# Second feed-forward layer as three rounded products, with its input split on GpSimd, in a four-phase layer

## The chip, the cores and the metric

One Trainium2 chip, one of its cores. The metric is the device time of one execution in microseconds, the median of several runs. A profiled execution gives a trace: each instruction's start and length on TensorE (PE), VectorE (DVE), ScalarE (ACT), GpSimd (POOL) and the DMA queue of SyncE (SP).

## The reference

The input is 16 batches of 1024 tokens of 256 numbers. Four residual blocks follow one another, each behind a layer norm: a state-space layer, the feed-forward block, an attention layer, the feed-forward block again. The change is in the feed-forward block only:

```python
    gf = _global_net(x.mean(axis=1, keepdims=True), ...)   # one number per batch
    out = x
    for _ in range(3):
        h = _gelu(out @ w1 + b1)      # 256 -> 256
        h = _gelu(h @ w2 + b2)        # 256 -> 128, the layer that is changed
        h = _gelu(h @ w3 + b3)        # 128 -> 64
        tf = sigmoid(h @ w4 + b4)     # 64 -> 1
        coupling = 0.1 + adaptive_range * (0.7 * gf + 0.3 * tf - 0.5) * 2.0
        out = out + coupling * _twist(out)
```

`_twist` permutes the four quarters of a token's vector and changes two signs, so the kernel keeps `out @ w1` (u) and `twist(out) @ w1` (v) beside one another and rotates those two from cycle to cycle instead of multiplying by `w1` again.

## The kernel before

Each feed-forward phase runs 8 steps; a step takes two batches, cut into four chunks of 512 tokens (`CHAINS` = 4, the `c` of the code). Three cycles of four chunks make 12 slots a step (`SLOTS`, the `m` of the code); slot m is chunk m % 4 in cycle m // 4. Two slots make a pair. All engines run instruction streams that are written out in the order of `step`, and meet at counting semaphores. Each engine takes its instructions strictly in order.

A slot goes as follows. TensorE turns u with eight transposes into `turned_ps` (`turn`, L1088). ScalarE applies Gelu to its two halves (`gelu1`, L976) into `h1[k]`, one of two buffers. TensorE multiplies by w2 in full float32 (`layer2`, L1097; a float32 product is issued as two instructions, so there are four a slot), and ScalarE applies the second Gelu (`gelu2`, L968). For each pair of slots there follow `layer3` (L1106), `gelu3` (L953), `layer4` (L1115), `tanh` (L960) and, on VectorE, `couple` (L804 to L814). Behind it VectorE rotates u and v of the two chunks with `rotate` (L823) and in the first cycle `rotate_other` (L832), eight instructions each a pair; the next cycle's `turn` of those chunks waits for it. After `turn` of slot m TensorE can run at most one second layer behind.

In slots 2 to 9 the step also prepares the next step's four chunks, one in two slots: `turn_z` (L1057), `high` on ScalarE and `low` on VectorE (L791), which split the normalised input into a rounded part and a rest, then `both_products` (L1072): 24 products of rounded (fp32r) operands, three terms for each half of the 256 inputs and each of four tiles. The products stand at the end of slots 3, 5, 7 and 9.

GpSimd computes scale factors (`rstds`, L691 to L695) from VectorE's `measure`, products of the couplings (`after_two`, L702 to L705), and, when the third coupling of a pair of chunks is known, the combined factors (L713 to L721) and the part of the output that the input itself gives (`base`, L727 and four tensor_scalars of 128x256 at L729 for each chunk). VectorE's `finish` (L844, L846) adds the rest, and SP stores. `base` of chunks 2 and 3, and `finish` of all four, stand in the next step. Before the change `base(it, s, j)` did the combination and both chunks of pair j in one go. SP's queue holds stores and loads in a written order, two chunks at a time.

`moments` and `std` have three sets of buffers for chunk 0 and two for the others; VectorE waits for `base` of the step that used the set before (L771).

Of the kernel before, what the change touches and what calls it, by code (L numbers as in the profile page):

```python
# [10 lines left out]
F32 = mybir.dt.float32  # L11
# [495 lines left out]
def ffn_semaphores(sem):  # L507
# [3 lines left out]
             "turned h1_ready h2_done h2_ready h3_done h3_ready token_done token_ready "  # L511
# [6 lines left out]
def ffn_phase(nc, sem, shared, start, name, identf, x1, x2, cn, gc, adaptive_range, early=None):  # L518
# [10 lines left out]
    with ExitStack() as ctx:  # L529
# [6 lines left out]
        def sems(names):  # L536
# [24 lines left out]
        zT_hi_other, zT_lo_other = sb("zT_hi_other", [P, KT, CH], F32R), sb("zT_lo_other", [P, KT, CH], F32R)  # L561
        h1 = [sb(f"h1_{k}", [P, KT, CH]) for k in range(2)]
        h2 = [sb(f"h2_{k}", [P, CH]) for k in range(2)]
        h3 = sb("h3", [P, CH])
        stats = [sb(f"stats{k}", [P, TT, 6]) for k in range(2)]
        moments = [[sb(f"moments{s}_{c}", [P, TT, 2]) for s in range(3 if c == 0 else 2)] for c in range(CHAINS)]
        std = [[sb(f"std{s}_{c}", [P, TT]) for s in range(3 if c == 0 else 2)] for c in range(CHAINS)]
# [24 lines left out]
         turned, h1_ready, h2_done, h2_ready, h3_done, h3_ready, token_done, token_ready,  # L592
         global_done, global_ready, kappa_pos, kappa_ready, coupling_ready, rotated,
         prod_ready, a_two_ready, prods_ready, b_pos_ready, a_std_ready, base_ready, y_ready) = counted
        w1_loaded, loaded, const_ready, weights_rounded, weights_ready, columns_ready = sems(
            "w1_loaded loaded const_ready weights_rounded weights_ready columns_ready")
# [35 lines left out]
        with nc.Block() as block:  # L632
# [45 lines left out]
            def _(pool):  # L678
# [29 lines left out]
                def base(it, s, j):  # L708
# [14 lines left out]
                    for k in range(2):  # L723
                        c = 2 * j + k
                        if not isinstance(it, int) or it > start:
                            pool.wait_ge(y_stored[c], 16 * it)
                        g.tensor_tensor(base_carrier[:, c:c + 1], base_ones[:, :], base_ones[:, :], ALU.mult)  # L727
                        for t in range(TT):
                            last = g.tensor_scalar(y[c][:, t, :], of_batch(z0, it, c)[:, t, :], a_std[j][:, t, k:k + 1],  # L729
                                                   of_batch(moments, it, c)[:, t, 0:1], ALU.mult, ALU.add)  # L730
                        last.then_inc(base_ready, 1)

                def step(it, s, first, second_last, last):
                    if first:
                        rstds(it + 1, 1 - s, 0)
                    if not last:
                        rstds(it + 1, 1 - s, 1)
                    if not first:
                        base(it - 1, 1 - s, 1)
                    if not last:  # L740
                        rstds(it + 1, 1 - s, 2)
                        rstds(it + 1, 1 - s, 3)
# [1477 lines left out]
```

## Time and profile before

| | |
|---|---|
| median of 3 runs | 3763.09 us (3757.67 to 3768.05) |
| profiled execution | 3763.16 us; span of its instructions 3761.3 us |
| mean granted TensorE clock, whole span | 0.978 |
| busy, share of the span | TensorE 95%, VectorE 79%, ScalarE 58%, GpSimd 44% |
| feed-forward phases | about 390 to 990 us and 3175 to 3758 us of the span |

"Busy" is the union of an engine's instructions in a stretch; the profile's length of a matmul overlaps that of the next one, so the price of a block of matmuls is read from the starts of two blocks. A granted clock of 1.00 is the full 2.4 GHz.

### The profile page before, as it was taken

To read this page: it belongs to the slowest core of one execution; us is meant where nothing else is said; L and a number is where in the kernel's file an instruction comes from. 1 tells how busy PE (TensorE), PEld (TensorE's weight loads), DVE (VectorE), ACT (ScalarE), POOL (GpSimd) and SP (SyncE) were. 2 spreads that over 40 slices of the span, in tenths; PEclk is the share of its full clock that TensorE was granted. 3 is DMA by queue.
4 is the path that set the end of the run, shared out by engine and by line. 5 is a ranking of instruction groups with operands and counts; after the bars stand their busy time and mean duration, and the time that the engine had idled before them with its cause. 6 is when DMAs were issued, how large, how long until landed. Compare 5 with 4: busy or idle time off the path is not lost. (4 is left out here: it accounts for less than half of the span.)

```text
span 3761.3 us, 76026 instructions
## 1 busy us (share of the span) xinstructions
PE 3560.0 (95%) x25550; PEld 2347.9 (62%) x25550; DVE 2952.9 (79%) x9275; ACT 2183.7 (58%) x4151; POOL 1666.4 (44%) x2027
## 2 busy tenths in 40 slices
PE   6999899999689999999999999999999998999997
PEld 5888666666455665566656656655666555666664
DVE  8998666766688888888888888888888893676775
ACT  1110456655337766766676667667667665656654
POOL 2332123223345556656555565565565511223323
PEclk9999899999879999999999999999999999999999
DMA  2333112111497978787887879788887832121211
GB/s 74 100 98 109 57 46 68 54 59 35 116 140 111 126 115 129 120 127 123 122 127 119 132 116 126 116 119 123 124 134 121 120 41 80 40 68 46 68 46 45
DMA packets 694291, 361.16 MB, mean 96 GB/s; under 512 B 297905, under 2 KB 660913, under 8 KB 693937
## 3 DMA queue, kind: packets, MB, share of 16 engines
q1 hardware_dynamic: 693936, 356.62, 53.5%
q8 instruction: 200, 3.28, 0.4%
q14 instruction: 155, 1.26, 0.2%
HBM read 204.49 MB, written 150.99 MB: 95 GB/s over the span
## 5 line engine op out<-in xcount | busy, mean ns | idle before, releaser
L1862 ACT ACTIVATE att_probs<-att_s 128x512 f32<-128x512 f32 x2304 | 1212.5, 601 | 461.2 <-PE att_s L2001 234.4
L1737 DVE CUSTOM_DVE_ANT_0 att_s<-att_s,att_above 128x384 f32<-128x384 f32 (+3 forms) x2048 | 950.2, 519 | 132.8 <-PE att_s L1981 127.1
L1981 PE MATMUL att_s<-att_ks,att_qs 48*128 48x512 f32 (+3 forms) x3072 | 896.0, 401 | 5.7 <-DVE att_maxima L1740 3.6
L2001 PE MATMUL att_s<-att_qs,att_ks 49*128 49x512 f32 (+3 forms) x3072 | 852.4, 373 | 20.5 <-DVE att_maxima L1737 5.2
L2001 PEld LDWEIGHTS att_s<-att_qs,att_ks 49*128 49x128 f32 x3072 | 487.6, 186 | 464.0 <-ACT att_probs L1862 271.6
L1740 DVE TENSOR_REDUCE att_maxima<-att_s 128x1 f32<-128x512 f32 x1024 | 661.9, 684 | 98.3 <-PE att_s L1981 93.2
L2029 PE MATMUL att_o_ps<-att_probs,att_vs 128*32 128x512 f32 (+3 forms) x6144 | 620.5, 497 | 25.1 <-ACT att_probs L1862 22.1
L1981 PEld LDWEIGHTS att_s<-att_ks,att_qs 48*128 48x128 f32 x3072 | 485.9, 189 | 26.4 <-DVE att_maxima L1737 8.9
L1097 PE MATMUL ffn_h2p<-ffn_h,ffn_w 128*128 128x512 f32 x768 | 365.0, 598 | 3.0 <-ACT ffn_h L968 0.9
L1951 PE MATMUL att_s<-att_mask,att_places 64*128 64x128 bf16 (+1 forms) x2560 | 327.7, 212 | 0.0
L1737 DVE DVE_READ_ACCUMULATOR2_ANT att_maxima<- 128x1 f32 x2048 | 293.0, 143 | 0.0
L946 ACT ACTIVATE ffn_uv<-ffn_uvp 128x512 f32<-128x512 f32 x256 | 153.1, 598 | 237.5 <-PE ffn_uvp L1072 237.5
L2029 PEld LDWEIGHTS att_o_ps<-att_probs,att_vs 128*32 128x32 f32 x6144 | 145.9, 108 | 222.9 <-issue 159.6
L1564 POOL CAST att_qs<-att_staged 113x1024 fp32r<-113x1024 f32 x128 | 253.7, 2005 | 0.0
L976 ACT ACTIVATE ffn_h<-ffn_turned,ffn_b 128x512 f32<-128x512 f32 x384 | 241.9, 684 | 13.5 <-PE ffn_turned L1088 11.6
L1564 POOL CAST att_ks<-att_staged 113x1024 fp32r<-113x1024 f32 x126 | 249.7, 2000 | 0.0
L968 ACT ACTIVATE ffn_h<-ffn_h2p,ffn_b 128x512 f32<-128x512 f32 x192 | 132.0, 687 | 197.8 <-PE ffn_h2p L1097 197.8
L1088 PEld LDWEIGHTS ffn_turned<-identf,ffn_uv 128*128 128x128 f32 x1536 | 174.8, 142 | 75.5 <-issue 53.9
L158 ACT ACTIVATE ssm_xnT<-ssm_turned 128x512 fp32r<-128x512 f32 x64 | 34.9, 595 | 313.7 <-PE ssm_turned L166 313.7
L1088 PE MATMUL ffn_turned<-identf,ffn_uv 128*128 128x128 f32 x1536 | 201.8, 274 | 10.2 <-DVE ffn_uv L823 8.0
L823 DVE SCALAR_TENSOR_TENSOR ffn_uv<-ffn_uv,ffn_c_pos 128x256 f32<-128x256 f32 x512 | 209.3, 483 | 2.3
L691 POOL TENSOR_TENSOR ffn_var_eps<-ffn_moments,ffn_eps 128x4 f32<-128x4 f32 x64 | 13.3, 208 | 433.4 <-DVE ffn_moments L776 433.4
(292 smaller groups left out, 6384.8 us busy)
## 6 DMA issues: line engine op xcount, KB each, us to landing
att_staged<-qk_scratch SPq DMA_DIRECT2D x768, 128.0 KB, 7.6
qk_scratch<-att_parts SPq DMA_DIRECT2D x128, 512.0 KB, 3.4
ffn_x<-x SPq DMA_DIRECT2D x64, 512.0 KB, 5.2
ssm_x<-in_L_attn_a_x_dram SPq DMA_DIRECT2D x32, 512.0 KB, 3.7
x<-ssm_y SPq DMA_DIRECT2D x32, 512.0 KB, 3.0
x<-ffn_y SPq DMA_DIRECT2D x32, 512.0 KB, 2.9
att_x<-x SPq DMA_DIRECT2D x32, 512.0 KB, 7.4
v_scratch<-att_v_tok SPq DMA_DIRECT2D x32, 512.0 KB, 5.3
```

The costliest lines, as they stand in the source:

```text
L823: last = v.scalar_tensor_tensor(out=new[:, t, 0:D], in0=old[:, t, D:2 * D], scalar=c_pos[i][j][:, t, k:k + 1], in1=old[:, t, 0:D], op0=ALU ...
L976: last = a(h1[k][:, f, :], turned_ps[:, f, :], ACT.Gelu, bias=b1[:, f:f + 1])
L1088: last = pe.transpose(turned_ps[:, f, t * P:(t + 1) * P], of[:, t, f * P:(f + 1) * P], identf[:, :])
L1097: last = mm(h2_ps[:, :], w2[:, f, :], h1[k][:, f, :], start=(f == 0), stop=(f == KT - 1))
L1564: last = g.tensor_copy(stack[0:ROWS, :].rearrange("p (t c) -> p t c", c=HD)[:, e * n:(e + 1) * n, :], staged[side][0:ROWS, :, e * n:(e + 1 ...
L1737: last = v.tensor_tensor_reduce(scores, scores, above[:, CH - w:CH], 1.0, -3.0e38, ALU.add, ALU.max, to)
L1740: last = v.tensor_reduce(to, scores, AX.X, ALU.max)
L1862: a(probs[u % PROBS][2 * g + p][:, 0:n], bank[:, 0:n], ACT.Exp).then_inc(exp_done, 1)
L1951: last = mm(blocks[:, at, GROUP * half:GROUP * (half + 1)], places[rows, 2 * (1 - k) + half, :], mask[rows, 1 - k, 0:len(cols), :], start= ...
L1981: last = mm(bank[:, col:col + w], rows_of(qs[buf], g, KROWS, p, BT * blk, BT * (blk + 1)), rows_of(ks[buf], g, KROWS, p, t0, t1), start=k ...
L2001: last = mm(bank[:, col:col + w], rows_of(ks[buf], g, SHIFT + 1, p, BT * j, BT * (j + 1)), rows_of(qs[buf], g, SHIFT + 1, p, t0, t1), star ...
L2029: last = mm(o_ps[32 * i:32 * i + 32, HD * (t0 - first_t):HD * (t1 - first_t)], vs[s][:, NBLK * head + j, :], probs[of % PROBS][i][:, col:c ...
```

## The change

The second layer becomes three rounded products, as the first already is: w2 is split once into `w2_hi` and `w2_lo` (two VectorE instructions before the first step), and h1 into `h1_hi` and `h1_lo` in every slot. For the first half of h1, ScalarE writes Gelu twice, once in float32 and once rounded. For the second half, GpSimd copies the float32 values into the rounded tile. GpSimd subtracts to give both low parts. A second layer is then six products instead of four instructions. GpSimd's order is written anew, with a split in every slot and the former `base` cut into `combine` and one `base` for each chunk. On TensorE `turn` comes ahead of `layer3` and `layer2`; ScalarE follows. On VectorE `finish` of chunk 1 and `normalise` of chunk 1 come two slots later, and `moments` and `std` get a third set for chunk 1.

```diff
@@ GpSimd @@
-                def base(it, s, j):
+                def combine(it, j):
...
                     pool.wait_ge(a_std_ready, n + 1)
-                    for k in range(2):
-                        c = 2 * j + k
...
+                def base(it, c):
+                    j, k = c // 2, c % 2
+                    if not isinstance(it, int) or it > start:
+                        pool.wait_ge(y_stored[c], 16 * it)
+                    g.tensor_tensor(base_carrier[:, c:c + 1], base_ones[:, :], base_ones[:, :], ALU.mult)
+                    for t in range(TT):
+                        last = g.tensor_scalar(y[c][:, t, :], of_batch(z0, it, c)[:, t, :], a_std[j][:, t, k:k + 1],
+                                               of_batch(moments, it, c)[:, t, 0:1], ALU.mult, ALU.add)
+                    last.then_inc(base_ready, 1)
+                def split(it, m):
+                    g1, k = SLOTS * it + m, m % 2
+                    for f in range(KT):
+                        if f == 0:
+                            pool.wait_ge(h1_high_ready, g1 + 1)
+                            if g1 >= 2:
+                                pool.wait_ge(h2_done, g1 - 1)
+                        else:
+                            pool.wait_ge(h1_ready, g1 + 1)
+                            g.tensor_copy(h1_hi[k][:, f, :], h1[k][:, f, :]).then_inc(h1_split, 1)
+                            pool.wait_ge(h1_split, 3 * g1 + 2)
+                        g.tensor_tensor(h1_lo[k][:, f, :], h1[k][:, f, :], h1_hi[k][:, f, :].bitcast(F32),
+                                        ALU.subtract).then_inc(h1_split, 1)
                 def step(it, s, first, second_last, last):
...
+                    for m in range(SLOTS):
+                        split(it, m)
+                        if m == 0 and not last:
+                            rstds(it + 1, 1 - s, 1)
+                        if m == 0 and not first:
+                            base(it - 1, 1)
+                        if m == 1 and not first:
+                            combine(it - 1, 1)
+                            base(it - 1, 2)
+                        if m == 2 and not first:
+                            base(it - 1, 3)
+                        if m in (4, 6) and not last:
+                            rstds(it + 1, 1 - s, m // 2)
+                        if m in (7, 9):
+                            after_two(it, (m - 7) // 2)
+                        if m == 10 and not second_last:
+                            rstds(it + 2, s, 0)
+                    combine(it, 0)
+                    base(it, 0)
@@ VectorE @@
-                        if m == 0 and not first:
+                        if m == 2 and not first:
                             finish(it - 1, 1 - s, 1)
...
-                        if m == 1 and not last:
+                        if m == 3 and not last:
                             normalise(it + 1, 1 - s, 1)
...
+                v.tensor_copy(w2_hi[:, :, :], w2[:, :, :]).then_inc(w2_rounded, 1)
...
+                v.tensor_tensor(w2_lo[:, :, :], w2[:, :, :], w2_hi[:, :, :].bitcast(F32), ALU.subtract).then_inc(columns_ready, 1)
@@ ScalarE, gelu1 @@
-                    for f in range(KT):
+                    for f in parts:
                         act.wait_ge(turned, KT * g + f + 1)
                         if f == 0 and old:
+                            act.wait_ge(h1_split, 3 * (g - 1))
                             act.wait_ge(h2_done, g - 1)
                         last = a(h1[k][:, f, :], turned_ps[:, f, :], ACT.Gelu, bias=b1[:, f:f + 1])
-                    last.then_inc(h1_ready, 1)
+                        if f == 0:
+                            a(h1_hi[k][:, f, :], turned_ps[:, f, :], ACT.Gelu, bias=b1[:, f:f + 1]).then_inc(h1_high_ready, 1)
+                        else:
+                            last.then_inc(h1_ready, 1)
@@ ScalarE, order in step: odd slots, then even slots @@
+                            gelu1(it, m, old, (0,))
                             if pair is not None:
                                 gelu3(it, pair, not first or pair > 0)
...
+                            gelu1(it, m, old, (1,))
                             if pair is not None:
                                 tanh(it, pair, not first or pair > 0)
...
+                            gelu2(it, m - 1, not first or m >= 3)
...
+                            gelu1(it, m, old)
                             if m:
                                 gelu2(it, m - 1, not first or m >= 3)
@@ TensorE, layer2 @@
-                    pe.wait_ge(h1_ready, g + 1)
+                    pe.wait_ge(h1_high_ready, g + 1)
...
                     for f in range(KT):
-                        last = mm(h2_ps[:, :], w2[:, f, :], h1[k][:, f, :], start=(f == 0), stop=(f == KT - 1))
+                        if f:
+                            pe.wait_ge(h1_split, 3 * g + 2)
+                        mm(h2_ps[:, :], w2_hi[:, f, :], h1_hi[k][:, f, :], start=(f == 0), stop=False)
+                        mm(h2_ps[:, :], w2_lo[:, f, :], h1_hi[k][:, f, :], start=False, stop=False)
+                    for f in range(KT):
+                        if f:
+                            pe.wait_ge(h1_split, 3 * g + 3)
+                        last = mm(h2_ps[:, :], w2_hi[:, f, :], h1_lo[k][:, f, :], start=False, stop=(f == KT - 1))
@@ TensorE, order in step: odd slots, then even slots @@
-                            if pair is not None:
-                                layer3(it, pair, first and pair == 0)
...
                             turn(it, s, m, False)
+                            if pair is not None:
+                                layer3(it, pair, first and pair == 0)
...
                             layer2(it, m - 1, first and m == 1)
...
+                            turn(it, s, m, first and m == 0)
                             if m:
                                 layer2(it, m - 1, False)
...
-                            turn(it, s, m, first and m == 0)
```

## Rows read from the trace of the kernel before

**Rows 1.** The page's first part: busy us, share of the span, instructions.
```profile
PE 3560.0 (95%) x25550; PEld 2347.9 (62%) x25550; DVE 2952.9 (79%) x9275; ACT 2183.7 (58%) x4151; POOL 1666.4 (44%) x2027
```
**Rows 2.** Stretches, busy PE PEld DVE ACT POOL, clock, DMA: step, its boundary, its rest.
```profile
3323.05:3394.80 71.75, 71.53 (x363) 49.54 (x362) 49.37 (x159) 43.61 (x84) 22.80 (x52) 1.00 0.19 59
3394.80:3418.00 23.20, 22.98 (x122) 14.08 (x120) 10.89 (x43) 15.71 (x30) 12.17 (x33) 1.00 0.16 49
3418.00:3466.40 48.40, 47.45 (x237) 34.44 (x236) 38.49 (x110) 27.41 (x53) 9.66 (x20) 1.00 0.21 65
```
**Rows 3.** Timeline of TensorE: start us, us, engine line operation out<-in xcount.
```profile
3394.69 1.88 PE L1097 MATMUL ffn_h2p<-ffn_h,ffn_w 128*128 128x512 f32 x4
...
3404.84 1.07 PE L1088 MATMUL ffn_turned<-identf,ffn_uv 128*128 128x128 f32 x8
...
3415.41 1.04 PE L1088 MATMUL ffn_turned<-identf,ffn_uv 128*128 128x128 f32 x8
3416.28 1.88 PE L1097 MATMUL ffn_h2p<-ffn_h,ffn_w 128*128 128x512 f32 x4
3418.00 0.95 PE L1115 MATMUL ffn_tp<-ffn_w,ffn_h 128*128 128x2 f32 x8
3418.81 0.71 PE L1072 MATMUL ffn_uvp<-ffn_wuv_hi,ffn_zT_hi 128*128 128x512 f32 x2
3419.36 0.62 PE L1072 MATMUL ffn_uvp<-ffn_wuv_lo,ffn_zT_hi 128*128 128x512 f32 x2
3419.82 0.62 PE L1072 MATMUL ffn_uvp<-ffn_wuv_hi,ffn_zT_lo 128*128 128x512 f32 x2
```
**Rows 4.** Timeline of ScalarE, the first Gelus of slot 0; in brackets idle time before.
```profile
3405.52 1.26 ACT L976 ACTIVATE ffn_h<-ffn_turned,ffn_b 128x512 f32<-128x512 f32 x2 [0.23 <-PE ffn_turned L1088]
```
**Rows 5.** Timeline of GpSimd in the attention phase.
```profile
1128.76 0.61 POOL L1550 CAST att_xnT<-att_full 128x512 fp32r<-128x512 f32 x1 [3.67 <-ACT att_full L1872]
1129.45 1.27 POOL L1552 TENSOR_TENSOR att_xnT<-att_full,att_xnT 128x512 fp32r<-128x512 f32 x1
1130.69 0.18 POOL L1562 TENSOR_TENSOR att_pool_carrier<-att_eps 1x1 f32<-1x1 f32 x1
```
**Rows 6.** Timeline of GpSimd around step boundaries of the second feed-forward phase.
```profile
3402.93 0.36 POOL L713 TENSOR_TENSOR ffn_prod_a<-ffn_c_pos,ffn_b_two 128x8 f32<-128x8 f32 x1 [6.22 <-DVE ffn_c_pos L814]
...
3405.09 2.15 POOL L729 TENSOR_SCALAR ffn_y<-ffn_z,ffn_a_std,ffn_moments 128x256 f32<-128x256 f32 x4
3407.22 0.18 POOL L727 TENSOR_TENSOR ffn_base_carrier<-ffn_base_ones 1x1 f32<-1x1 f32 x1
3407.39 2.15 POOL L729 TENSOR_SCALAR ffn_y<-ffn_z,ffn_a_std,ffn_moments 128x256 f32<-128x256 f32 x4
...
3466.88 0.20 POOL L691 TENSOR_TENSOR ffn_var_eps<-ffn_moments,ffn_eps 128x4 f32<-128x4 f32 x1 [3.90 <-DVE ffn_moments L776]
...
3468.24 0.20 POOL L695 TENSOR_TENSOR ffn_std<-ffn_var_eps,ffn_rstd 128x4 f32<-128x4 f32 x1
```
**Rows 7.** Timelines of GpSimd and VectorE where both work, in two steps.
```profile
3349.26 3.13 POOL L729 TENSOR_SCALAR ffn_y<-ffn_z,ffn_a_std,ffn_moments 128x256 f32<-128x256 f32 x4
3349.40 4.05 DVE L823 SCALAR_TENSOR_TENSOR ffn_uv<-ffn_uv,ffn_c_pos 128x256 f32<-128x256 f32 x8
...
3419.57 2.35 DVE L814 TENSOR_SCALAR ffn_c_pos<-ffn_tanh_token,ffn_ar_cols,ffn_kappa 128x8 f32<-128x8 f32 x1
3419.74 2.15 POOL L729 TENSOR_SCALAR ffn_y<-ffn_z,ffn_a_std,ffn_moments 128x256 f32<-128x256 f32 x4
3421.96 3.26 DVE L823 SCALAR_TENSOR_TENSOR ffn_uv<-ffn_uv,ffn_c_pos 128x256 f32<-128x256 f32 x8
```
**Rows 8.** Timeline of TensorE in slots 4 and 5.
```profile
3424.36 0.60 PE L1057 MATMUL ffn_zTp<-identf,ffn_z 128*128 128x128 f32 x4
3424.80 1.88 PE L1097 MATMUL ffn_h2p<-ffn_h,ffn_w 128*128 128x512 f32 x4
...
3429.05 0.66 PE L1057 MATMUL ffn_zTp<-identf,ffn_z 128*128 128x128 f32 x4 [0.48 <-DVE ffn_zT_lo L791]
```

More of the change, by code:

```diff
@@ L565, in ffn_phase @@
         stats = [sb(f"stats{k}", [P, TT, 6]) for k in range(2)]
-        moments = [[sb(f"moments{s}_{c}", [P, TT, 2]) for s in range(3 if c == 0 else 2)] for c in range(CHAINS)]
-        std = [[sb(f"std{s}_{c}", [P, TT]) for s in range(3 if c == 0 else 2)] for c in range(CHAINS)]
+        moments = [[sb(f"moments{s}_{c}", [P, TT, 2]) for s in range(3 if c < 2 else 2)] for c in range(CHAINS)]
+        std = [[sb(f"std{s}_{c}", [P, TT]) for s in range(3 if c < 2 else 2)] for c in range(CHAINS)]
         var_eps = sb("var_eps", [P, TT])
@@ L735, in step @@
                         rstds(it + 1, 1 - s, 0)
[L736 to L742, printed above, removed]
-                    after_two(it, 0)
-                    after_two(it, 1)
-                    if not second_last:
-                        rstds(it + 2, s, 0)
-                    base(it, s, 0)
+                    for m in range(SLOTS):
[17 more added lines that the diff above has]
+                    base(it, 0)
                 for c in range(CHAINS):
@@ L751, in _ @@
                 steps(step)
-                base(end - 1, 1, 1)
+                base(end - 1, 1)
+                combine(end - 1, 1)
+                base(end - 1, 2)
+                base(end - 1, 3)
             @block.vector
@@ L994, in step @@
                         if m % 2:
+                            if m == 1:
+                                context(it, 2)
+                            if c is not None:
+                                high(it + 1, c, 1, True)
+                            gelu1(it, m, old, (0,))
                             if pair is not None:
@@ L998, in step @@
                                 gelu3(it - 1, PAIRS - 1, True)
-                            if m == 1:
-                                context(it, 2)
-                            if c is not None:
-                                high(it + 1, c, 1, True)
-                            gelu1(it, m, old)
-                            gelu2(it, m - 1, not first or m >= 3)
+                            gelu1(it, m, old, (1,))
                             if pair is not None:
@@ L1149, in step @@
                             turn(it, s, m, False)
+                            if pair is not None:
+                                layer3(it, pair, first and pair == 0)
+                            elif not first:
+                                layer3(it - 1, PAIRS - 1, False)
                             layer2(it, m - 1, first and m == 1)
```

33 lines of the change are left out of this document (13 added, 20 removed).

## The prediction

> **What bounds the kernel now.** I read the page's first part, then stretches of one feed-forward step, then timelines of its engines. Over the whole span TensorE is busy 95% and GpSimd 44% [rows 1], but that mixes four phases. The change touches the two feed-forward phases alone, so I cut out one step of the second (12 slots, 71.75 us): TensorE is busy 71.53 us of it, VectorE 49.37, ScalarE 43.61, GpSimd 22.80 [rows 2]. TensorE sets the pace and its clock stands at 1.00. A step has two unlike stretches. From the end of the products of slot 9 (3394.69, where the next second layer starts) to the end of slot 2's second layer (3418.00) TensorE has no products to do: 23.3 us with the six second layers of slots 9, 10, 11, 0, 1 and 2 [rows 3]. I call it the boundary. The other stretch, 48.4 us, holds the four blocks of products and the other six. In the boundary GpSimd is already busy 12.17 of 23.20 us, in the rest 9.66 of 48.40 [rows 2].
>
> **What the change takes off TensorE.** The second layer takes 1.72 us a slot now: it starts at 3416.28 and the next work at 3418.00 [rows 3]. Six rounded products replace it. Two such products take 0.46 us (3419.36 to 3419.82) [rows 3], so six take 1.38: 0.34 us less a slot, 4.1 us a step, 65 us over 192 slots if TensorE stays the bound. That is the whole prize. The reordering and the other edits on TensorE issue the same instructions.
>
> **What it adds to GpSimd.** Each slot gets a subtraction, a copy and a subtraction of 128x512. GpSimd does the same pair in the attention phase: copy at 1128.76, wait, subtraction at 1129.45, next instruction at 1130.69 [rows 5]: 1.93 us, and 1.24 for another subtraction. A split is 3.17 us, 38.0 us a step. With the 22.8 us of before GpSimd needs 60.8 us of a step that TensorE could do in 67.6. On the average it fits. The order decides whether it does.
>
> **Where it doesn't fit.** GpSimd takes its work in order, and each second layer waits for its own split (all but the first two of its six products need it). Between the start of split 10 and the end of split 2 the new order on GpSimd holds: split 10, scale factors of the batch after next, split 11, combine and base 0, split 0, scale factors, base 1, split 1, combine and base 2, split 2. Prices: combine with one base 4.29 us (3402.93 to 3407.22), a base alone 2.32 (3407.22 to the end of its four at 3409.54), scale factors 1.56 (3466.88 to 3468.44) [rows 6]. Sum: 5 x 3.17 + 2 x 1.56 + 2 x 4.29 + 2.32 = 29.9 us. Nothing in it waits long for another engine: turn m needs only split m-2, and each coupling is ready before its combine's turn comes. It begins when ScalarE has written the first half of slot 10 twice: 0.68 us from the transposes' start to the first Gelu and 1.26 for two [rows 3, 4], so 2.0 us after the products of slot 9. After its end one wake and one product, 0.3 us. Boundary after: 32.2 us against 23.3, **+8.9 us**. TensorE waits in order in front of the products of slot 3, so it cannot use that time. Before, the combine and bases stood there too, but nobody waited on GpSimd for them; now each has a second layer queued behind it.
>
> In the other stretch six second layers save 6 x 0.34 = **-2.0 us**. There GpSimd keeps up: seven splits are 22.2 us, and with at most the 9.66 us of before [rows 2] that is 31.9 of 46.4.
>
> **Sharing between GpSimd and VectorE.** This is the unknown size. Four GpSimd tensor_scalars took 3.13 us instead of 2.15 when eight VectorE operations with two inputs ran at the same time, and those 4.05 instead of 3.26 [rows 7]: 0.25 us lost by GpSimd and 0.20 by VectorE for each GpSimd instruction of 0.54. At 3419.57 a small VectorE operation stood 2.35 us, until four GpSimd ones had ended (3419.74 to 3421.89) [rows 7]. So a subtraction of 1.28 us costs VectorE between 0.47 (the first case by length) and 1.28 (the second); I take 0.9, and 0.2 for the copy: 2.0 us a split, and three times 0.25 us of GpSimd's own. In the boundary two splits meet VectorE's finish: +1.5 (bounds 0 and 3). In the rest the place that matters is behind slot 3: base 3 and split 3 come late, beside the 6.5 us of rotations, and half of split 4 too: VectorE is 1.5 x 2.0 = 3.0 us later. Against that, its coupling ended 3.1 us after layer 4 before (3421.92 against 3418.81 [rows 3, 7]), held up by bases; now base 3 ends 2.32 us after split 2, that is 1.2 after layer 4 (0.35 and 0.81 come between), and 0.3 for the coupling makes 1.5. Net 1.4 later. TensorE comes for the low half 4.7 us after the products before, 0.48 of it idle (3424.36, 3429.05 [rows 8]); now 0.44 + 0.87 + 1.38 = 2.7 after [rows 3, 8], since layer 3 follows instead. VectorE is there at 4.7 + 1.4 = 6.1, so 3.4 us idle instead of 0.5; with about 0.5 each at slot 7 and at two even slots, +4 (bounds 0 and 8).
>
> The Trainium skill (SBUF — State Buffer, Who interferes with whom) says that the two engines' shared port is an exclusive lock: the one that starts second is blocked for the whole instruction. The 2.35 us agree; the 4.05 us don't, since 2.15 and 3.26 us one behind the other would be 5.41. By the rule to the letter every split would cost VectorE its full length; that is the third rival.
>
> **Edits at nothing.** ScalarE's third Gelu of a slot, 0.58 us, is 7 us a step; it has 71.75 - 43.61 = 28 us free [rows 2]. If that cover went, it would cost at most 7 us a step. Rounding w2 is two VectorE operations a phase, ahead of the first step, while TensorE still does products. The third set of moments removes a VectorE wait that no TensorE wait follows. Finish 1 and normalise 1 come two slots later; their stores, and the loads behind them in SP's queue, serve the step after next, so their cover is most of a step, 71.75 us; without it a store of a few us would show.
>
> **Sum.** A step: 8.9 + 1.5 - 2.0 + 4 = +12.4 us. There are 7 boundaries and 7 stretches with products in each of two phases: 14 x 12.4 = +174. The last step of a phase has no products; in its slots 3 to 11 GpSimd has 9 x 3.17 us of splits, a base and little else, 33 us, about what is left for TensorE there: +3 for waits, an estimate. Bases 0 to 3 come one behind the other at the end, +2; the phase's first slots -1. That is +4 a phase, +8 (bounds 0 and 16). The profiled execution took 3763.16 us (span 3761.3), 0.07 from the median of 3763.09. Forecast: 3763 + 182 = **3945 us**, slower by 4.8%.
>
> **Rivals.**
> 1. *The split keeps up* (faster). The boundary would be TensorE's, and 65 us come back less the ends' 8: 3706. It decides at the price of a split: the step breaks even, without sharing, at 2.0 + 5s + 14.0 + 0.3 = 23.3 + 2.0, s = 1.8 us, which needs subtractions as fast as copies. Against it: 3.17 us [rows 5], in a form and size that are the same. For it: GpSimd's total fits. Chance 0.08, and 0.02 that it ends within the bound of no change.
> 2. *Pile-up without sharing.* Both engines interleave at no cost: 14 x 6.9 = 97, and nothing at the ends: 3860. For it, many of the splits in the products' stretch fall beside VectorE work with one input. Against it: rows 7. Chance 0.12.
> 3. *Full lock.* Each split costs VectorE 3.2 us and GpSimd a whole VectorE operation per instruction: about 9 in place of 4, 4 in place of 1.5, 14 x 19.9 + 16 = 295: 4058. For it the 2.35 us; against it the 4.05. Chance 0.10.
> 4. *ScalarE becomes the bound.* 43.6 + 7.0 = 50.6 of at least 67 us a step; even if all of it showed, 16 x 7.0 = 112: 3875. Chance under 0.01.
>
> **How the numbers follow.** My forecast, pile-up with partial sharing, has 0.68: 3900 to 3990 by half the way to the bounds. With bounds of 0 and 8, 0 and 3 the step lies between +6.9 and +17.9: 3763 + 97 and 3763 + 251 + 16, that is 3860 to 4030. The second rival's time lies at the low end and most of the third's above the high end. The range is 3850 to 4035. About 0.3% (11 us) is what a measurement of this kernel can tell from no change; faster 0.08, same 0.02, slower 0.90.
>
> **What the profile would show.** Right: 1152 second-layer products that start 0.23 us apart; GpSimd subtractions near 1.28 us and copies near 0.61; TensorE idle behind the GpSimd split, ten us a step, all near the step boundary in slots 0 to 3; GpSimd without a gap there; VectorE rotations stretched behind slot 3. Wrong: GpSimd idle in the boundary (an order or a wait I misread); subtractions well under 1.2 us; idle TensorE spread evenly over all slots, which would be latency and not pile-up; or TensorE's clock falling in its new pauses, which would make the time longer still: it stood at 1.00 through all three stretches [rows 2], and how it takes pauses of some 4 us no row of that stretch shows.

## The result and the profile after

The kernel after takes 3989.24 us (median of 4 runs, 3981.61 to 3995.01) against 3760.53 for the kernel before: a ratio of 1.0606, 95% interval 1.0587 to 1.0624. The prediction said 3945 (3850 to 4035); the change costs 229 us where 182 were forecast. The profiled execution took 3989.59 us, its span 3987.8.

The page's first part for the kernel after; [rows 1] hold the same for before.

```profile
PE 3642.1 (91%) x25934; PEld 2490.7 (62%) x25934; DVE 3166.0 (79%) x9279; ACT 2284.6 (57%) x4343; POOL 2297.0 (58%) x2603
```

GpSimd is busy 631 us more (16 steps of 38.0 make 608), and VectorE, which got no new work in the loop, 213 us more. The next fence holds stretches of a steady step of the second phase, from the end of slot 9's products to the same point a step later, then its boundary and its rest (columns as in [rows 2]).

```profile
3537.40:3622.75 85.35, 76.13 (x382) 57.43 (x381) 64.93 (x153) 49.45 (x95) 60.23 (x88) 0.90 0.16 50
3537.40:3569.78 32.38, 26.86 (x133) 18.98 (x132) 20.84 (x46) 19.11 (x36) 28.96 (x52) 0.84 0.17 51
3569.78:3622.75 52.97, 49.27 (x250) 38.45 (x249) 44.09 (x107) 30.34 (x59) 31.27 (x37) 0.94 0.16 49
```

The step went from 71.75 to 85.35 us [rows 2]: the boundary from 23.20 to 32.38, the rest from 48.40 to 52.97. VectorE is busy 64.93 us of it instead of 49.37. TensorE is idle 9.2 us instead of 0.2, of which 5.5 in the boundary and 3.7 in the rest, and its busy time went up, though its products take less: the granted clock is 0.90, and 0.84 in the boundary.

TensorE in slots 1 to 7 of that step (start, us; in brackets idle time before and what ended it) answers to [rows 3, 8]:

```profile
3560.61 0.80 PE L1136 MATMUL ffn_h2p<-ffn_h_hi,ffn_w_hi 128*128 128x512 f32 x1 [2.20 <-POOL ffn_h_hi L747]
...
3568.09 0.50 PE L1136 MATMUL ffn_h2p<-ffn_h_hi,ffn_w_hi 128*128 128x512 f32 x1 [1.69 <-POOL ffn_h_hi L747]
...
3570.59 1.02 PE L1109 MATMUL ffn_uvp<-ffn_wuv_hi,ffn_zT_hi 128*128 128x512 f32 x2
3571.41 1.05 PE L1109 MATMUL ffn_uvp<-ffn_wuv_lo,ffn_zT_hi 128*128 128x512 f32 x2
...
3581.72 0.66 PE L1094 MATMUL ffn_zTp<-identf,ffn_z 128*128 128x128 f32 x4 [1.12 <-DVE ffn_zT_lo L820]
...
3597.65 0.71 PE L1094 MATMUL ffn_zTp<-identf,ffn_z 128*128 128x128 f32 x4 [2.46 <-DVE ffn_zT_lo L820]
3598.15 1.91 PE L1125 MATMUL ffn_turned<-identf,ffn_uv 128*128 128x128 f32 x8
```

In the boundary TensorE waits for the split; in the rest it waits for VectorE's low half. Behind such pauses the first pairs of products of slot 3 start 0.82 us apart instead of 0.55, and eight transposes take 1.91 instead of 1.07 [rows 3]. A short stretch of slot 3 shows why (columns as above): the granted clock is 0.50, that is 1.2 GHz.

```profile
3571.40:3573.10 1.70, 1.70 (x5) 1.32 (x4) 1.70 (x1) 0.22 (x1) 1.70 (x3) 0.50 0.12 37
```

GpSimd: the first instruction of split 10, the last of split 2, and the start of split 6; then VectorE in slots 5 and 6 (both answer to [rows 5, 7]).

```profile
3539.48 1.28 POOL L749 TENSOR_TENSOR ffn_h_lo<-ffn_h,ffn_h_hi 128x512 fp32r<-128x512 f32 x1 [5.14 <-issue]
...
3568.11 1.28 POOL L749 TENSOR_TENSOR ffn_h_lo<-ffn_h,ffn_h_hi 128x512 fp32r<-128x512 f32 x1
...
3594.93 3.19 POOL L749 TENSOR_TENSOR ffn_h_lo<-ffn_h,ffn_h_hi 128x512 fp32r<-128x512 f32 x1 [5.70 <-ACT ffn_h_hi L1011]
```

```profile
3586.61 3.09 DVE L814 TENSOR_SCALAR ffn_z<-ffn_x,ffn_moments,ffn_rstd 128x256 f32<-128x256 f32 x4
...
3590.56 3.26 DVE L852 SCALAR_TENSOR_TENSOR ffn_uv<-ffn_uv,ffn_c_pos 128x256 f32<-128x256 f32 x8
3593.74 3.25 DVE L861 SCALAR_TENSOR_TENSOR ffn_uv<-ffn_uv,ffn_c_neg 128x256 f32<-128x256 f32 x8
```

From 3539.48 to 3569.39 are 29.9 us, the sum of the prediction to the tenth. In this stretch GpSimd's instructions took their price; it was VectorE's that were stretched (four instructions of normalise 2.65 and 3.19 us, 1.38 before). The 3.19 us subtraction started under VectorE's rotations and ended 1.1 us after them (3596.99); VectorE's normalise, 3.09 us for four, ran beside split 5.

The last step of the second phase, from the end of slot 9's products to the end: before, then after.

```profile
3682.30:3757.90 75.60, 58.20 (x280) 33.58 (x278) 43.05 (x126) 36.29 (x63) 27.59 (x74) 0.92 0.14 48
```

```profile
3879.37:3984.40 105.03, 67.09 (x310) 47.92 (x308) 51.97 (x126) 43.53 (x77) 79.43 (x116) 0.75 0.10 34
```

So this end costs 29.4 us more, where the prediction had a boundary (10.4) and 5. The first phase's end costs the same (29.5, up to the last product).

### The profile page after: what moved, and what is told of

Its sections match the earlier page's. It is cut to its first block and busy times, and to the rows that moved or that the text cites. A ratio compares the mean times of both kernels' runs of the same rounds, so it can differ in the third digit from the quotient of the medians.

```text
span 3987.8 us, 77690 instructions
## 1 busy us (share of the span) xinstructions
PE 3642.1 (91%) x25934; PEld 2490.7 (62%) x25934; DVE 3166.0 (79%) x9279; ACT 2284.6 (57%) x4343; POOL 2297.0 (58%) x2603
## 3 DMA queue, kind: packets, MB, share of 16 engines
q14 instruction: 163, 1.34, 0.2%
## 5 line engine op out<-in xcount | busy, mean ns | idle before, releaser
L749 POOL TENSOR_TENSOR ffn_h_lo<-ffn_h,ffn_h_hi 128x512 fp32r<-128x512 f32 x384 | 540.6, 1411 | 370.7 <-ACT ffn_h_hi L1011 185.8
L1009 ACT ACTIVATE ffn_h<-ffn_turned,ffn_b 128x512 f32<-128x512 f32 x384 | 265.6, 692 | 51.3 <-PE ffn_turned L1125 50.8
L1125 PE MATMUL ffn_turned<-identf,ffn_uv 128*128 128x128 f32 x1536 | 236.6, 305 | 32.9 <-DVE ffn_uv L852 29.0
L1136 PE MATMUL ffn_h2p<-ffn_h_hi,ffn_w_hi 128*128 128x512 f32 x384 | 186.6, 486 | 61.1 <-POOL ffn_h_hi L747 58.8
L1125 PEld LDWEIGHTS ffn_turned<-identf,ffn_uv 128*128 128x128 f32 x1536 | 203.6, 160 | 45.6 <-DVE ffn_uv L852 29.7
L852 DVE SCALAR_TENSOR_TENSOR ffn_uv<-ffn_uv,ffn_c_pos 128x256 f32<-128x256 f32 x512 | 222.4, 503 | 2.3
L843 DVE TENSOR_SCALAR ffn_c_pos<-ffn_tanh_token,ffn_ar_cols,ffn_kappa 128x8 f32<-128x8 f32 x96 | 63.6, 663 | 197.2 <-ACT ffn_tanh_token L992 197.2
```

Source lines behind the costliest of these rows:

```text
L749: g.tensor_tensor(h1_lo[k][:, f, :], h1[k][:, f, :], h1_hi[k][:, f, :].bitcast(F32), ALU.subtract).then_inc(h1_split, 1)
L852: last = v.scalar_tensor_tensor(out=new[:, t, 0:D], in0=old[:, t, D:2 * D], scalar=c_pos[i][j][:, t, k:k + 1], in1=old[:, t, 0:D], op0=ALU ...
L1009: last = a(h1[k][:, f, :], turned_ps[:, f, :], ACT.Gelu, bias=b1[:, f:f + 1])
L1125: last = pe.transpose(turned_ps[:, f, t * P:(t + 1) * P], of[:, t, f * P:(f + 1) * P], identf[:, :])
```

## The experiments

All were timed beside the kernel before; the table has each one's median, its ratio to the kernel before and the 95% interval of that. Differences between two experiments are taken from their ratios, times 3762 us. The code is cut to the lines that matter. "The rival" is the second outcome that each expectation names. Only split on VectorE, bases spread, fillers, old orders and orders only compute the whole; the others leave out the low half of the layer's input.

| kernel | us | ratio | interval |
|---|---|---|---|
| products only | 3711 | 0.9862 | 0.9840 to 0.9885 |
| one write | 3762 | 1.0005 | 0.9990 to 1.0019 |
| half twice | 3780 | 1.0048 | 1.0030 to 1.0066 |
| orders only | 3797 | 1.0089 | 1.0060 to 1.0118 |
| no split | 3808 | 1.0117 | 1.0093 to 1.0141 |
| slow powers | 3863 | 1.0265 | 1.0242 to 1.0287 |
| powers waited | 3905 | 1.0402 | 1.0357 to 1.0448 |
| split on VectorE | 3923 | 1.0430 | 1.0396 to 1.0463 |
| fillers | 3985 | 1.0580 | 1.0559 to 1.0601 |
| unread split | 3989 | 1.0608 | 1.0570 to 1.0646 |
| old orders | 4030 | 1.0711 | 1.0687 to 1.0734 |
| bases spread | 4069 | 1.0803 | 1.0772 to 1.0835 |

**Orders only.**

```diff
-mm(h2_ps[:, :], w2_hi[:, f, :], h1_hi[k][:, f, :], start=(f == 0), stop=False)
-mm(h2_ps[:, :], w2_lo[:, f, :], h1_hi[k][:, f, :], start=False, stop=False)
-split(it, m)
+last = mm(h2_ps[:, :], w2[:, f, :], h1[k][:, f, :], start=(f == 0), stop=(f == KT - 1))
```

> The kernel after, with the second layer back as four float32 products and without the split and the second write of ScalarE; every new order stays (TensorE, ScalarE, VectorE, GpSimd's bases between the slots). Theory of the prediction (GpSimd's split is what costs): the orders by themselves cost nothing, 3763 us, 3750 to 3775. Rival (the orders cost: layer 3 ahead of the second layer leaves VectorE less time for the low half, and the bases come later): the products' stretch keeps most of its 4.6 us a step, 14 x 3.5 = 49: about 3810 us.

3797 us: between the two, +33 us. A step takes 72.4 us on the mean of twelve instead of 71.7; from the last products to the end of a phase it is 13 to 14 us more, most of the 33 (what goes on there is shown below). The prediction had the orders at nothing.

**No split.**

```diff
-split(it, m)
+a(h1_hi[k][:, f, :], turned_ps[:, f, :], ACT.Gelu, ...)      # both halves a second time
+last = mm(h2_ps[:, :], w2_hi[:, f, :], h1_hi[k][:, f, :], ...)  # third pair
```

> All of the change without the split: six rounded products a slot stay, ScalarE writes both halves a second time, the products with the low half take the high half in its place, GpSimd does nothing for it (this leaves the low half of the input out of the computation). It shows the prize by itself. If TensorE sets the pace: 0.34 us a slot less, 192 slots, 65 us: 3698 us, 3685 to 3715. Rival (a chain through ScalarE's Gelus sets the pace once TensorE is faster, so that little of the prize can be had even with no split): 3740 us or more.

3808 us, slower than before with GpSimd's part gone, as the rival said. TensorE's greatest waits in 340 us, 4.7 steps (us, times, longest):

```profile
PE ffn_turned L1124 <- ACT ffn_h_hi L1008: 12.0, 23, 0.8
PE ffn_tp L1174 <- ACT ffn_g L1020: 4.2, 4, 1.2
```

The transposes of the next slot wait until ScalarE has read their bank (the buffer that the transposes write) for the last time, 2.6 us a step.

**Unread split.**

```diff
-g.tensor_tensor(h1_lo[k][:, f, :], h1[k][:, f, :], h1_hi[k][:, f, :].bitcast(F32), ALU.subtract)
+g.tensor_tensor(h1_lo[k][:, f, :], wuv_lo[:, f, :].bitcast(F32), wuv_hi[:, f, :].bitcast(F32), ALU.subtract)
+last = mm(h2_ps[:, :], w2_hi[:, f, :], h1_hi[k][:, f, :], ...)   # third pair, as in no split
```

> As the kernel without the split, but GpSimd does the same three instructions of 128x512 a slot, at the same places of its queue and after the same Gelus, on weights and into a tile that nobody reads: GpSimd's load and its sharing with VectorE without any wait of TensorE or ScalarE for it (the low half is left out of the computation). Theory of the prediction (the queue costs, sharing is the smaller part): the boundary is TensorE's again; VectorE stays late by some 4 us a step, and 5 us at each phase's end: 3698 + 14 x 4 + 10 = about 3765 us, 3740 to 3800. Rival (sharing is the greater part: VectorE held up by GpSimd makes TensorE wait wherever it comes from): 3860 us or more.

3989 us, as the kernel after, though neither TensorE nor ScalarE waits for the split anywhere: the rival is right, and the prediction's theory fell as a complete account. TensorE's greatest wait in one step, and VectorE's rotations behind slot 3:

```profile
PE ffn_zTp L1092 <- DVE ffn_zT_lo L818: 8.1, 2, 7.9
```

```profile
3571.68 5.26 DVE L850 SCALAR_TENSOR_TENSOR ffn_uv<-ffn_uv,ffn_c_pos 128x256 f32<-128x256 f32 x8
3576.87 8.00 DVE L859 SCALAR_TENSOR_TENSOR ffn_uv<-ffn_uv,ffn_c_neg 128x256 f32<-128x256 f32 x8
```

TensorE passes the boundary early, and base 3 with splits 3 and 4 then meet rotations that take 13.2 us instead of 6.5. The low half is 7.9 us late.

**Bases spread.**

```diff
+if m == 1: combine(it - 1, 0); base(it - 1, 1)
+if m == 3: combine(it - 1, 1); base(it - 1, 2)
+if m == 5: base(it - 1, 3); base(it - 1, 0)
```

> The kernel after with GpSimd's other work moved out of the boundary: combine 0 and base 1 behind split 1, combine 1 and base 2 behind split 3, bases 3 and 0 behind split 5, scale factors behind splits 2, 4, 6 and 9; finishes, stores and loads follow that order. Nothing is left out. Theory of the queue: between the start of split 10 and the end of split 2 stand now 5 x 3.17 + 4.29 = 20.1 us instead of 29.9, the boundary falls from 32.4 to about 23.5 us: 14 x 8.9 = 125 less, 3864 us, and down to 3820 if TensorE's clock, with fewer pauses, stays at 1.00 behind slot 3. Rival (sharing): the same GpSimd work only meets VectorE in another place, 3950 to 4000 us.

4069 us, beyond even the rival. From the start of slot 9's last product to that of slot 3's first there are 27.0 us instead of 33.4, 6.4 of the 8.9 us that were worked out, but the step is 91.5 us. Waits of TensorE in 340 us, some 3 steps:

```profile
PE ffn_zTp L1091 <- DVE ffn_zT_lo L817: 24.7, 7, 5.1
...
PE ffn_uvp L1106 <- DVE ffn_zT_lo L817: 8.7, 5, 2.8
...
PE ffn_h2p L1133 <- POOL ffn_h_hi L742: 1.5, 3, 0.5
```

The wait for the split is gone but for 1.5 us, and that for VectorE's low half is 33.4 us, against 14.0 in 340 us, 4 steps, of the kernel after.

**Products only.**

```diff
-last = mm(h2_ps[:, :], w2[:, f, :], h1[k][:, f, :], start=(f == 0), stop=(f == KT - 1))
+mm(h2_ps[:, :], w2_hi[:, f, :], h1[k][:, f, :], start=(f == 0), stop=False)    # h1 is rounded
+mm(h2_ps[:, :], w2_lo[:, f, :], h1[k][:, f, :], start=False, stop=False)
+last = mm(h2_ps[:, :], w2_hi[:, f, :], h1[k][:, f, :], start=False, stop=(f == KT - 1))
```

> The kernel before with one edit: its second layer is six rounded products, and ScalarE writes its input once, rounded; the third pair takes that rounded input again (the low half of the input is left out of the computation). Orders, GpSimd, VectorE and ScalarE as before. It gives TensorE's prize with nothing else. If TensorE sets the pace all through: 0.34 us less in each of 192 slots, 3763 - 65 = 3698 us, 3688 to 3712. Rival (with a shorter second layer another chain sets the pace: ScalarE's Gelu of one slot ahead of the transposes of the next, or VectorE's low half): 3730 us or more.

3711 us: 52 of the 65 us, at the upper end of what was expected if TensorE sets the pace. The step is 68.6 us; VectorE's low half is waited for a little (6.6 us in five steps). It is faster than both kernels, but it is not the whole computation.

**Slow powers.**

```diff
-g.tensor_tensor(h1_lo[k][:, f, :], wuv_lo[:, f, :].bitcast(F32), wuv_hi[:, f, :].bitcast(F32), ALU.subtract)
+g.tensor_tensor(slow_out[k][:, 2 + 5 * f:7 + 5 * f], slow[:, 2:7], slow[:, 2:7], ALU.pow)
```

> As the kernel with the unread split (3989 us), but GpSimd's three instructions a slot are powers on 128x5, 128x2 and 128x5: about as long on GpSimd (a power on 128x4 takes 1.01 us in the kernel), at the same places, with hardly an element read or written (the low half is left out of the computation). It parts GpSimd's time from its sharing with VectorE. Theory of sharing (VectorE is held up by what GpSimd reads and writes): back to near the kernel without the split, 3808 to 3840 us. Rival (GpSimd's queue alone: its bases and scale factors come late behind the splits, and VectorE waits for them): 3920 us or more.

3863 us, between the two. The powers took 1277 and 723 ns, no less than the subtraction and copy. GpSimd's time alone costs 56 us over the kernel without the split; its reads and writes cost another 129.

**Fillers.**

```diff
+fill((0, 16, 12)[m] if m in (1, 2) else 0)    # layer2, ahead of the wait for the split's copy
+fill({5: 8, 7: 18}.get(m, 0))                 # ahead of turn_z in odd slots
```

> The kernel after with useless products in the four longest pauses of TensorE in a step: 16 and 12 of 240 columns between the two halves of the second layers of slots 1 and 2, 8 and 18 ahead of the transposes in slots 5 and 7. A steady step after has 9.2 us of idle TensorE and 76.1 us busy, where 67.4 were worked out for a full clock: 8.7 us are the half clock behind pauses. Theory of the clock (pauses cost a second time, behind them): the half clock behind slot 3 and in slot 7 goes, 2 x 1.7 us a step at the least, 14 x 3.4 = 48: 3940 us, and down to 3870 if all 8.7 us come back. Rival (the half clock only fills time that GpSimd and VectorE would make TensorE wait anyway): 3980 to 4010 us.

3985 us, as the rival said. Three steps of the first phase (the useless products count as busy):

```profile
519.83:603.75 83.92, 79.82 (x436) 63.44 (x436) 65.98 (x151) 49.19 (x95) 60.11 (x89) 0.94 0.14 45
...
771.34:855.33 83.99, 77.17 (x437) 60.57 (x436) 63.19 (x153) 49.01 (x95) 62.49 (x90) 0.98 0.19 57
855.33:940.44 85.11, 79.51 (x435) 62.25 (x436) 64.23 (x152) 49.01 (x95) 59.81 (x89) 0.94 0.12 38
```

The clock rose from 0.90 to 0.94 and 0.98, and the step fell by 0.2 to 1.4 us, not with the clock. The useless products did not hold TensorE up: in the second of these steps each of the four rows of them is followed by a wait again, 1.34 and 0.45 us for VectorE's low half, 1.08 and 1.38 for the split's copy.

**Old orders.**

```diff
+layer3(it, pair, first and pair == 0)
 turn(it, s, m, False)
-layer3(it, pair, first and pair == 0)
 layer2(it, m - 1, first and m == 1)
```

> The kernel after with the orders of before on TensorE and ScalarE (layer 3 ahead of the transposes, the second layer ahead of them in even slots, both Gelus of a slot together); the split, the second write and GpSimd's new order stay. Theory (orders and split add up): the 34 us of the orders by themselves come back: 3955 us, 3940 to 3970. Rival (the new orders are what gives the split its time: in even slots the second layer is then asked for a transpose earlier, 1 us, in six slots a step): 14 x 6 = 84 more than that, 4040 us.

(Odd slots are shown; in even slots the second layer goes ahead of the transposes, and ScalarE's order follows.) 4030 us, close to the rival: orders and split don't add up. The orders by themselves cost 33 us, yet taking them back costs some 40 more (1.0711 against 1.0606): in the orders of before the split costs more. That the new ones give it time is the rival's reason and was not measured by itself.

**One write.**

```diff
-a(h1[k][:, f, :], turned_ps[:, f, :], ACT.Gelu, ...)
 last = a(h1_hi[k][:, f, :], turned_ps[:, f, :], ACT.Gelu, ...)
```

> As the kernel with all of the change but the split (3808 us), with ScalarE writing its rounded output once instead of twice (the low half is left out of the computation). The new orders and the six products, and nothing else. If the parts add up: 3763 + 34 (orders alone) - 52 (products alone, in the orders of before) = 3745 us, 3735 to 3757, and ScalarE's second write is what took the other 60. Rival (in the new orders TensorE waits for ScalarE's Gelus anyway): 3785 us or more.

3762 us, between the two: with the new orders the six products give back 32 us of 65 (orders only to one write).

**Powers waited.**

```diff
+pe.wait_ge(h1_split, 3 * g + 2); pe.wait_ge(h1_split, 3 * g + 3)
+act.wait_ge(h1_split, 3 * (g - 1)); pool.wait_ge(h2_done, g1 - 1)
```

> As the kernel with the slow powers (3863 us: GpSimd's time without its reads and writes), but TensorE, ScalarE and GpSimd wait for each other at the powers exactly as they do at the split in the kernel after (the low half is left out of the computation). It is the queue of the prediction without sharing. If the waits add to GpSimd's lateness: the boundary, 26.5 us between products there, goes to the 33.4 of the kernel after, 14 x 6.9 = 97 more: 3960 us. Rival (they are the same lateness, seen by TensorE in one place or by VectorE in another; it is sharing that makes up the rest): 3863 to 3910 us.

3905 us: the rival, at its upper end. Without sharing the waits cost 52 us over the slow powers, not 97. One step of each phase:

```profile
515.71:594.60 78.89, 71.93 (x383) 55.13 (x382) 48.24 (x152) 56.04 (x107) 57.40 (x89) 0.96 0.17 54
3342.63:3424.44 81.81, 74.54 (x381) 56.55 (x382) 48.55 (x152) 55.57 (x107) 56.92 (x89) 0.92 0.17 52
```

VectorE is back at 48.2 to 48.6 us. The two steps differ by 2.92 us, 2.61 of it in TensorE's busy time at a lower clock: here, where VectorE is not late, half clock seems to show in the time. That was not tried by itself.

**Split on VectorE.**

```diff
+a(h1_hi[k][:, f, :], h1[k][:, f, :], ACT.Copy)                       # ScalarE rounds
+v.tensor_tensor(h1_lo[k][:, f, :], h1[k][:, f, :], h1_hi[k][:, f, :], ALU.subtract)
```

> A whole version with nothing left out: orders of before on TensorE, six rounded products, ScalarE rounds both halves by a copy from its own output (not from the transposes' bank), VectorE subtracts them (128x512 each), in even slots last and in odd slots behind the first rotation; GpSimd as before. VectorE's load goes from 49.4 to about 49.4 + 24 x 0.65 = 65 us of a step of 68.7 (the step with the products alone). Theory of sharing (without GpSimd's accesses nothing is stretched, an engine can be filled to 95%): 3711 + 14 x 2 = 3740 us, 3715 to 3765. Rival (the order counts: a queue in which second layers wait behind finishes and rotations costs as GpSimd's did): 3800 us or more.

3923 us, as the rival said. It beats the kernel after by 1.7% and stays behind the kernel before. VectorE is busy 63.35 of 82.00 us, so there was room; TensorE's second layers waited for the low half from VectorE, which comes at its place in VectorE's queue (19.4 us in 340, four steps; 2.5 at the longest).

**Half twice.**

```diff
-split(it, m)
+last = mm(h2_ps[:, :], w2_hi[:, f, :], h1_hi[k][:, f, :], ...)  # three Gelus a slot stay
```

> The kernel after with GpSimd's part left out and nothing else: ScalarE writes three Gelus a slot as in the kernel after (the first half twice, the second half once, rounded), TensorE multiplies six times and waits for ScalarE alone, the third pair takes the high halves (the low half is left out of the computation). What stands between this kernel and the kernel after is GpSimd's split and its waits. One write gave 3762 us, two full writes 3808. If ScalarE's writes cost in proportion: 3785 us, and GpSimd's part is 204 of the 226. Rival (only the second half's second write holds up the transposes of the next slot; the kernel after shows 0.3 us of that wait a step): 3762 + 14 x 0.3 = 3766 us, 3755 to 3775, and GpSimd's part is 223 of them.

3780 us, between the two, nearer to the first. GpSimd's split and its waits are 0.0558 of 3762, 210 us. A steady step:

```profile
3435.52:3507.36 71.84, 69.50 (x382) 54.21 (x382) 48.97 (x152) 49.00 (x95) 21.84 (x53) 0.98 0.19 59
```

That is as long as before [rows 2], with shorter products: TensorE idles 2.3 us. Its wait for the bank of the transposes is 0.4 us a step, so of the 16 us that the third Gelu costs (one write to half twice) that wait explains some 6; where the rest lies was not traced.

**What VectorE pays.** Groups of VectorE's instructions by line (busy us, mean ns, idle before) in the kernel after, then half twice, then the waited powers:

```profile
L852 DVE SCALAR_TENSOR_TENSOR ffn_uv<-ffn_uv,ffn_c_pos 128x256 f32<-128x256 f32 x512 | 222.4, 503 | 2.3
L814 DVE TENSOR_SCALAR ffn_z<-ffn_x,ffn_moments,ffn_rstd 128x256 f32<-128x256 f32 x256 | 179.5, 761 | 13.0 <-POOL ffn_rstd L695 12.6
L873 DVE SCALAR_TENSOR_TENSOR ffn_y<-ffn_z,ffn_b_pos,ffn_y 128x128 f32<-128x128 f32 x256 | 135.3, 529 | 27.2 <-POOL ffn_y L733 26.6
...
L843 DVE TENSOR_SCALAR ffn_c_pos<-ffn_tanh_token,ffn_ar_cols,ffn_kappa 128x8 f32<-128x8 f32 x96 | 63.6, 663 | 197.2 <-ACT ffn_tanh_token L992 197.2
```

```profile
L851 DVE SCALAR_TENSOR_TENSOR ffn_uv<-ffn_uv,ffn_c_pos 128x256 f32<-128x256 f32 x512 | 208.4, 479 | 2.3
...
L813 DVE TENSOR_SCALAR ffn_z<-ffn_x,ffn_moments,ffn_rstd 128x256 f32<-128x256 f32 x256 | 96.1, 437 | 9.8 <-POOL ffn_rstd L695 9.3
L872 DVE SCALAR_TENSOR_TENSOR ffn_y<-ffn_z,ffn_b_pos,ffn_y 128x128 f32<-128x128 f32 x256 | 91.9, 359 | 24.8 <-POOL ffn_y L733 24.2
...
L842 DVE TENSOR_SCALAR ffn_c_pos<-ffn_tanh_token,ffn_ar_cols,ffn_kappa 128x8 f32<-128x8 f32 x96 | 31.2, 325 | 199.8 <-ACT ffn_tanh_token L991 199.7
```

```profile
L815 DVE TENSOR_SCALAR ffn_z<-ffn_x,ffn_moments,ffn_rstd 128x256 f32<-128x256 f32 x256 | 94.4, 430 | 18.2 <-POOL ffn_rstd L697 17.7
...
L844 DVE TENSOR_SCALAR ffn_c_pos<-ffn_tanh_token,ffn_ar_cols,ffn_kappa 128x8 f32<-128x8 f32 x96 | 28.8, 300 | 216.2 <-ACT ffn_tanh_token L993 216.1
```

The instructions of normalise (`ffn_z<-ffn_x`), the same at the same places, take 437 ns on the mean without a split, 430 beside powers, 761 beside the split. What GpSimd reads and writes stretches VectorE, not that GpSimd is busy. From half twice to the kernel after, normalise grows by 83 us, the half of finish shown (`ffn_y`) by 43, the coupling shown (`ffn_c_pos`) by 32 and the rotations shown (`ffn_uv`) by 14: in the kernel after, the rotations behind slot 3, on which the prediction laid most of the sharing, belong to the group that pays least.

**The last step.** In half twice it takes 86.98 us (to be held against 75.60 and 105.03):

```profile
3696.82:3783.80 86.98, 61.78 (x310) 46.40 (x308) 42.93 (x126) 43.74 (x77) 28.14 (x74) 0.82 0.12 41
```

So 11.4 of the 29.4 us are there without any split, and the split takes 18.0. TensorE's waits from the last products to the end, in the kernel after, then from somewhat earlier in half twice:

```profile
PE ffn_turned L1125 <- DVE ffn_uv L852: 14.4, 4, 5.3
PE ffn_h2p L1136 <- POOL ffn_h_hi L747: 7.1, 4, 2.9
PE ffn_h2p L1141 <- POOL ffn_h_lo L749: 1.6, 4, 0.4
```

```profile
PE ffn_turned L1125 <- DVE ffn_uv L851: 10.1, 4, 2.7
```

Before, it was 4.0 us in 4 waits for the rotations. In the old orders a second layer of 1.72 us stands between layer 4, which starts the coupling, and the next transposes; in the new ones nothing does. That is 6.1 of the 11.4 us; the mean clock, 0.82 against 0.92, is another part, not priced by itself. And this is where GpSimd is held up worst:

```profile
3916.24 3.24 DVE L861 SCALAR_TENSOR_TENSOR ffn_uv<-ffn_uv,ffn_c_neg 128x256 f32<-128x256 f32 x8
...
3921.25 0.33 DVE L875 SCALAR_TENSOR_TENSOR ffn_y<-ffn_z,ffn_b_neg,ffn_y 128x128 f32<-128x128 f32 x1
```

```profile
3917.28 5.43 POOL L749 TENSOR_TENSOR ffn_h_lo<-ffn_h,ffn_h_hi 128x512 fp32r<-128x512 f32 x1 [4.02 <-ACT ffn_h_hi L1011]
```

A subtraction of 1.28 us stood 5.43: it ended 1.13 us after the last of VectorE's back-to-back operations with two inputs (3921.58). It happens again 15 us later (5.42).

## Why the prediction came out as it did

The time lies inside the range, and the queue on GpSimd is what the prediction said it is. But the step of the sum that the queue should explain came out by sharing as well, and two errors of opposite sign stand in the total. In part it is luck.

**The boundary: right in size, incomplete in cause.** Forecast 32.2 us and 1.5 for sharing, measured 32.38; the queue from split 10 to split 2 is 29.9 us in both, so of the 1.5 nothing showed. TensorE's waits there are 5.5 us, not ten: some 6 us more went into products at a lower clock (26.86 us busy, where 22.98 - 2.0 = 20.9 were its work). That clock, 0.84, is one of the prediction's own signs of being wrong; since GpSimd worked through its queue without a gap, it cost nothing here that the queue did not cost anyway. But what stands in the boundary is not what the change would give back without it. The unread split and the spread bases both took most or all of the waits for the split away, and the time stayed or rose. GpSimd's work then meets VectorE's rotations. The prediction added queue and sharing as two terms; they stand in for each other. Beside powers the waits add 52 us (slow powers to waited powers), beside whole tiles none (unread split to the kernel after, 3989 each, the latter with one Gelu a slot less).

**The rest: right in cause, wrong in its parts.** Forecast 50.4, measured 52.97. VectorE's low half is late in slots 5 and 7, for 1.12 and 2.46 us where 3.4 and about 0.5 were forecast: split 5 stretched normalise to 3.09 us ahead of slot 7's rotations, and nothing in the sum stood for that. In all TensorE idles 3.70 us instead of 0.95, 2.75 more where 4 were forecast. The other 3.9 us are busy time at half clock (49.27, where 47.45 - 2.0 = 45.4 were its work), which the prediction named and did not price. With the clock raised the time hardly moved, so in this kernel it fills what VectorE would take anyway.

**Sharing: the partial one.** VectorE grew by 64.93 - 48.97 = 16.0 us a step (half twice to after), 1.3 us a split; the prediction took 2.0 (0.47 to 1.28 a subtraction), and its full lock 3.2. Single instructions go beyond a full lock (a subtraction that stood 5.43 us); the rotations that took 8.00 us beside four subtractions and two copies got on meanwhile. The Trainium skill (SBUF — State Buffer, Who interferes with whom) calls the two engines' shared port an exclusive lock, held for a whole instruction. The 5.43 us are longer than that, since the subtraction waited for a row of instructions, and the mean of 1.3 us is less than a split's 3.2. In time: waited powers to after 0.0204, 77 us, where the forecast had 14 x 5.5 = 77 in the steps. That agreement is partly luck, since the waited powers hold one more Gelu a slot.

**TensorE's prize and the edits at nothing: wrong.** The prediction credited 65 us and put orders and the third Gelu at nothing. Products only gave 52; in the new orders 32 were left, the orders themselves cost 33, and the third Gelu 16 (one write to half twice). Without GpSimd the change is +18 us, not -65. The cover named for the Gelu, 28 us of free ScalarE, was not enough: where both halves are written twice (no split), the bank of the transposes stays occupied while ScalarE reads it once more, 2.6 us a step, and a part of the 16 is that wait. The cover of the orders was not looked at in the last step, where no products hide VectorE's rotations.

**The split and its waits: overrated.** 182 + 65 = 247 us forecast, 210 measured. Errors of 83 us (18 instead of -65) and 37 us in opposite directions leave the 47 that the total is off.

**Where the 47 lie.** Twelve steps of 13.6 us more instead of 12.4: 14. From a phase's first products to the end of slot 9's it is about 3 us more, where -2.0, +4 and -1 make 1: 4 in both phases. The last steps: 29.4 instead of 15.4 a phase, 28 us. Of that 28, 23 stand in half twice (11.4 a phase) and belong to the edits at nothing; the rotations that lost their cover are 6.1 of each 11.4. The split's own part is 18.0 a phase, 2.6 more than forecast: "+3 for waits, an estimate" counted GpSimd's 33 us of splits and not a subtraction stuck behind VectorE.

**The rivals.** That the split keeps up is excluded by 29.9 us. Pile-up without sharing was put at 3860; built, it took 3905, with the orders and one more Gelu a slot in it, which the rival had at nothing. Full lock, 4058, is ruled out for the whole; single instructions meet it or go beyond it. ScalarE is not the bound: it is busy 49.45 of 85.35 us.

## What to carry to other kernels

Before work goes to an idle engine, look at who shares its access to memory: the same microseconds on GpSimd cost 56 us with hardly an element touched and 185 with whole tiles. A wait that is removed from one place can come back at another engine, as VectorE's low half did in the unread split and the spread bases, so measure the prize alone (products only) before paying for it. And price a new order in the stretch that has no long products, since that is where a lost cover shows.

## What the runs showed of the hardware

- GpSimd and VectorE hold each other up by what they read and write, not by being busy: powers of 1.28 us beside the same VectorE work cost it nothing (430 ns a normalise against 437), subtractions of 1.28 us made it 761.
- A GpSimd subtraction that begins under VectorE operations with two inputs can wait for the whole unbroken row of them: 5.43, 5.42 and 3.19 us instead of 1.28, each ending 1.1 us after the row.
- TensorE's granted clock fell to 0.50 behind pauses of 2.20 and 2.46 us. Behind one of 1.69 us it first stood at 1.00 and fell at slot 3's first products. From 3546.90 to 3549.20 of the same step it was 0.50 too, though no pause since the end of slot 9's products (3537.40) was longer than 0.36 us. The mean of a step went from 1.00 to 0.90. With most of the four longest pauses filled by useless products it was 0.94 to 0.98, and the time stayed.
